# Attention and gated feed-forward on one core: the first head's probability sum gets a place of its own, the next tokens are prepared a unit earlier, two output tiles move into a batch's last unit, and the last key tile's denominators come from its probabilities

## The reference

```python
x = x + _attention(_tc_rmsnorm(x, t, g1w, g1b, b1w, b1b), Wq, Wk, Wv, Wo)
return x + _swiglu(_tc_rmsnorm(x, t, g2w, g2b, b2w, b2b), gate_w, hid_w, out_w)
# _tc_rmsnorm: g * x * rsqrt(mean(x * x) + EPS) + b, with g and b from t
# _attention: 16 heads of 32; softmax(q k / sqrt(32)) v, then Wo
# _swiglu: silu(x @ gate_w.T) * (x @ hid_w.T) @ out_w.T, hidden width 2048
```

## Time and profile before

| | |
|---|---|
| median of 3 runs | 2479.52 us (2472.38 to 2492.58) |
| the profiled execution | 2483.76 us, its span 2481.9 us |
| mean granted TensorE clock | 0.976 |
| busy share of the span | PE 93%, PEld 63%, DVE 68%, ACT 53%, POOL 59% |
| first exponential of batches 0 to 3 | 94.52, 445.95, 795.53, 1143.42 us |
| last exponential of batches 0 to 3 | 378.72, 730.17, 1078.31, 1423.99 us |

### The profile page before, as it was taken

The page is one execution under the profiler, slowest core; times in us unless marked ns, Lnnn a source line. Parts: engine busy times, 40 slices in busy tenths (PEclk is TensorE's granted clock), DMA queues, the critical chain, the costliest instruction groups (busy, mean ns, idle before and its releaser), DMA issues. The chain is left out here.

```text
span 2481.9 us, 40287 instructions
## 1 busy us (share of the span) xinstructions
PE 2309.7 (93%) x10884; PEld 1572.9 (63%) x10884; DVE 1676.2 (68%) x2732; ACT 1310.9 (53%) x2319; POOL 1454.4 (59%) x1351
## 2 busy tenths in 40 slices
PE   5999989999989999989999848999999999999999
PEld 4655436554447555456554336888888888888887
DVE  4776734667725776537777347887788778778877
ACT  3366762566752667734667724445444534454454
POOL 0388981689970888944889925731572166216711
PEclk8999999999989999999999978999999999999999
DMA  5212203212122122132222043115412541254125
GB/s 179 81 41 63 64 14 108 52 41 67 48 71 64 38 69 52 47 95 52 51 57 60 21 162 136 60 60 179 151 54 69 170 154 52 74 164 157 47 81 174
DMA packets 92656, 209.60 MB, mean 84 GB/s; under 512 B 15632, under 2 KB 15632, under 8 KB 90640
## 3 DMA queue, kind: packets, MB, share of 16 engines
q1 hardware_dynamic: 91344, 202.71, 27.2%
q0 software_dynamic: 1088, 4.19, 0.4%
HBM read 134.23 MB, written 19.92 MB: 62 GB/s over the span
## 5 line engine op out<-in xcount | busy, mean ns | idle before, releaser
L680 DVE TENSOR_REDUCE pmax<-bank 128x1 f32<-128x512 f32 x1024 | 653.7, 684 | 197.0 <-PE bank L893 187.6
L599 ACT ACTIVATE probs<-bank 128x512 f32<-128x512 f32 x1024 | 572.0, 600 | 330.6 <-PE bank L973 249.5
L447 POOL TENSOR_TENSOR sums<-sums,probs 128x512 f32<-128x512 f32 x512 | 641.4, 1291 | 0.5 <-ACT probs L599 0.5
L447 POOL TENSOR_TENSOR sums<-probs 128x512 f32<-128x512 f32 x256 | 320.4, 1282 | 380.6 <-ACT probs L599 258.9
L973 PE MATMUL bank<-qs,ks 128*128 128x512 f32 x1024 | 441.3, 439 | 40.0 <-ACT probs L599 37.9
L893 PE MATMUL bank<-ks,qs 96*128 96x512 f32 x1024 | 402.9, 406 | 25.8 <-DVE pmax L680 25.1
L973 PEld LDWEIGHTS bank<-qs,ks 128*128 128x128 f32 x1024 | 192.8, 191 | 323.4 <-ACT probs L599 167.3
L1536 PE MATMUL bank<-H_hi,wt_hi 128*128 128x512 f32 x896 | 350.0, 391 | 14.6 <-DVE H_lo L1391 14.6
L1550 PE MATMUL bank<-ow,aw 128*128 128x512 f32 x1536 | 358.7, 392 | 0.0
L1536 PE MATMUL bank<-H_lo,wt_hi 128*128 128x512 f32 x896 | 349.6, 390 | 0.0
L1536 PE MATMUL bank<-H_hi,wt_lo 128*128 128x512 f32 x896 | 349.5, 390 | 0.0
(11 more groups left out here) (139 smaller groups left out, 3233.8 us busy)
## 6 DMA issues: line engine op xcount, KB each, us to landing
raw<-in_gu_w SPq DMA_DIRECT2D x66, 512.0 KB, 3.6
wo_raw<-in_out_w SPq DMA_DIRECT2D x128, 256.0 KB, 2.6
ks<-qk_hi SPq DMA_DIRECT2D x136, 128.0 KB, 2.4
qs<-qk_hi SPq DMA_DIRECT2D x264, 64.0 KB, 2.0
x<-in_x SPq DMA_DIRECT2D x10, 1024.0 KB, 5.2
ks<-qk_lo SPq DMA_DIRECT2D x68, 128.0 KB, 2.4
qs<-qk_lo SPq DMA_DIRECT2D x132, 64.0 KB, 2.0
wv<-wv_parts SPq DMA_DIRECT2D x4, 2048.0 KB, 8.9
```

Source lines behind the costliest of these rows:

```text
L447: nc.gpsimd.tensor_tensor(sums[:, h, :], first, probs[:, s % 2, h, :], ALU.add) \
L599: nc.scalar.activation(probs[:, s % 2, h, :], sbank[i % SB][:], ACT.Exp, scale=SCALE).then_inc(st_done, 1)
L680: nc.vector.reduce_max(pmax[:, t, h, hf:hf + 1], mbank[n % MB][:], AX_X).then_inc(sq_done, 1)
```

## The change

Four things are changed.

1. `sum_place`: in the first half of a unit the first head's sum goes to `yout[:, 0]`, in the second half to `sums[:, 0]`; so the first addition of a half no longer writes what the denominator matmuls read, and the wait for them goes from the first head to the second. At a batch's start the first addition waits for the store of the output tile that lay in `yout[:, 0]`. The squares' unused output goes to `qk_hi` instead of `yout`.
2. The next tokens' load, squares, roots, scaling and transposes stand about a unit earlier, and the projections that are in their way are drawn together.
3. Tiles 0 and 1 of the output projection are made in unit 7, two matmuls a step from q = 18 and q = 24. For this VectorE, not GpSimd, multiplies unit 6's output, in unit 7 at (3, 0), from a copy of `den` in the free bank `mspare`; the first three tiles of `o` are copied to that bank before they are split.
4. Unit 7's last key tile is not added by GpSimd: the denominators are made from the sum of key tiles 4 to 6 and, by four more matmuls, from the probabilities of tile 7; they stand ahead of output tiles 2 to 7, and VectorE does unit 7's multiplication too.

```diff
-HT_AT = {5: (9, 13, 17, 24), 7: (13, 16, 19, 23)}
+HT_AT = {(4, 15): (0, 0), (4, 18): (1, 0), (4, 24): (2, 0), (5, 8): (3, 0),
+         (6, 14): (0, 1), (6, 17): (1, 1), (6, 24): (2, 1), (7, 0): (3, 1)}
+EARLY_OUT = {18: 0, 24: 1}
+SPLIT_AT = {(3, 3): 0, (4, 1): 1, (7, 1): 2}
...
+    def sum_place(quad, h):
+        return yout[:, 0, :] if (quad, h) == (0, 0) else sums[:, h, :]
+
...
-                    if u == 3:
+                    if u == 1:
                         load_x(b, 0, prepared)
...
-                hold(sp, held, sum_done, sums_done(b, NU - 1, NS - 1, GH - 1))
+                hold(sp, held, w_ready, MISC(b, misc_index(True, ("D", NU - 1, 1)) + 1))
                 load_wv()
...
-                        if (u, s) == (4, 5):
+                        if (u, s) == (3, 6):
                             inverse_root(b, b * 2 + 2)
-                        if (u, s) == (6, 6):
+                        if (u, s) == (6, 0):
                             inverse_root(b, b * 2 + 3)
-                        if s == 4 and u:
+                        if s == 4 and 0 < u < NU - 1:
                             normalise(b, u - 1)
+                        if n == NU * NS - 1:
+
+                            pool.wait_ge(sum_done, sums_done(b, u, s - 1, GH - 1))
+                            pool.sem_inc(sum_done, GH)
+                            break
...
-                            if s % QT == 1 and h == 0:
+                            if (u, s, h) == (0, 1, 0):
+
+                                pool.wait_ge(y_stored[0], b * (NT // 2 * 16) + 16)
+                            if s % QT == 1 and h == 1:
 
                                 pool.wait_ge(w_ready, MISC(b, sums_before(u, s // QT)))
...
-                            first = probs[:, 0, h, :] if s % QT == 1 else sums[:, h, :]
-                            nc.gpsimd.tensor_tensor(sums[:, h, :], first, probs[:, s % 2, h, :], ALU.add) \
+                            total = sum_place(s // QT, h)
+                            first = probs[:, 0, h, :] if s % QT == 1 else total
+                            nc.gpsimd.tensor_tensor(total, first, probs[:, s % 2, h, :], ALU.add) \
                                 .then_inc(sum_done, 1)
...
-                normalise(b, NU - 1)
...
+                tokens = o[:, :, t * P:(t + 1) * P]
+                if t in SPLIT_AT.values():
+                    up = mspare[:].rearrange("p (g c) -> p g c", g=NG)
+                    if t:
+                        act.wait_ge(os_dve, b * NT + t)
+                    nc.scalar.activation(up, tokens, ACT.Copy).then_inc(o_up, 1)
+                    act.wait_ge(o_up, b * len(SPLIT_AT) + (t + 1))
+                    tokens = up
+                nc.scalar.activation(osplit[:, t % 2, 0, :, :], tokens, ACT.Copy).then_inc(os_act, 1)
+
+            def denominators_up(b):
+
+                act.wait_ge(den_ready, b * (NU - 1) + (NU - 1))
+                act.wait_ge(sq_done, SCORES_Q(b, (NU - 1) * NMAX + NMAX) + MB)
+                nc.scalar.activation(mspare[:], den[:], ACT.Copy).then_inc(den_up, 1)
...
-                            if (u, s) == (4, 4):
+                            if (u, s) == (3, 4):
                                 square(b, 0, h)
-                            if (u, s) == (4, 6):
+                            if (u, s) == (4, 1):
                                 scale_x(b, 0, h)
-                            if (u, s) == (6, 3):
+                            if (u, s) == (5, 5):
                                 square(b, 1, h)
-                            if (u, s) == (6, 7):
+                            if (u, s) == (6, 2):
                                 scale_x(b, 1, h)
...
-                for t in range(2):
-                    lo_part(t)
                 out_tile(0)
-                for t in range(2, 4):
-                    lo_part(t)
+                lo_part(len(SPLIT_AT))
                 work_tile(b, ("D", NU - 1, 1))
-                for part in range(3):
+                for part in range(4):
                     normalise(b, NU - 1, part)
...
+                direct = (u, quad) == (NU - 1, QUADS - 1)
+                pe.wait_ge(sum_done, sums_done(b, u, QT * quad + QT - 1 - direct, GH - 1))
                 for h in range(GH):
-                    last = nc.tensor.matmul(wbank[DH * h:DH * h + DH, :], ones[:], sums[:, h, :], start=True, stop=True)
+                    last = nc.tensor.matmul(wbank[DH * h:DH * h + DH, :], ones[:], sum_place(quad, h), start=True,
+                                            stop=not direct)
+                for h in range(GH if direct else 0):
+                    last = nc.tensor.matmul(wbank[DH * h:DH * h + DH, :], ones[:], probs[:, (NS - 1) % 2, h, :], start=False,
+                                            stop=True)
...
+                            for q, t in EARLY_OUT.items() if u == NU - 1 else ():
+                                step = s * GH + h - q
+                                if 0 <= step < NG * 3 // 2:
+                                    out_tile(b, t, slice(2 * step, 2 * step + 2))
```

104 lines of the change are left out of this document (66 added, 38 removed).

## The result

The changed kernel takes 2487.2 us (median of 20 runs, 2478.7 to 2495.5), the kernel before 2478.2 (median of 20, 2472.4 to 2492.6). The ratio is 1.003, with a 95% interval of 1.0019 to 1.0041: the change costs 0.3%, where 2419 us had been forecast. The profiled execution has a span of 2483.8 us.

The account below looks back on a forecast made before the run. Took GpSimd's closed loop of additions and waits for denominator reads as the bound, with TensorE nearly full; 29 (units 0 to 6) + 11.7 (last unit) + 17.2 (end) + 2 (half clock), 60 us off 2479.5: 2419 us, range 2392 to 2452.

Parts of the forecast that it names:

- the part on the next tokens: Units 3 to 6: next tokens' work about a unit earlier wins 0.8 - 0.3 + 1.4 + 2.0 = 3.9 us per batch.
- rival 3: Units 5 and 6 fall to half clock (1.2 GHz), 16 us more per unit, 128 in four batches: 2547 us; chance 0.04.
- the steps on part 1: GpSimd's loop shortens 1.82 us per unit; units 0, 1, 2 win 0.5 + 1.5 + 1.35 = 3.35 us.
- TensorE can follow only as far as its idle time goes: Caps the 1.82 us won in GpSimd's loop at TensorE's idle time: 1.51, 1.35 and 1.52 us in units 1, 2, 3.
- the shifted tiles: In unit 7, two output tiles enter (5.54 us), three transposed tiles leave (2.0): 34.2 us against a mean of 37.1.
- a rule against the row: The skill's rule, optimize the highest-occupancy engine first, makes relieving GpSimd (59%) worth nothing: 2450 us; the rows say 2419.
- Unit 4: Gets back 1.02 us from the root, takes on three transposed tiles (2.0): -0.3 us, between +0.2 and -2.5.
- Unit 7 and the end: Last unit wins 2.9 us per batch (11.7 in all), the batch's end 4.3 (17.2), tile 5 starting about 744.6.
- Rival 1: TensorE is the floor in units 0 to 6; only last unit and end win, 29 us: 2450 us; chance 0.20.
- rival 2: Everything overlaps: units win 1.8 each, last unit 4, end 6.6, about 85 us: 2395 us; chance 0.13.
- a bound for units 0 to 6: Upper bound of 12.5 us per batch (50 in all), if the full 1.82 comes in each of seven units.

Follow-up runs that it names:

- e7: e1's kernel with the parts of the query projections in units 0 and 2 two heads apart, as before the change: 2417.7 us, ratio 0.975.
- e1: The changed kernel with the mean square made by ScalarE behind its fourth square instead of by VectorE: 2431.0 us, ratio 0.980.
- e5: The kernel before with only the first head's sum in its own place, in units 0 to 3, 5 and 7: 2445.3 us, ratio 0.987.
- e4: The changed kernel with the first head's sum in the common place again, waiting for the denominators ahead of each half's first addition: 2466.0 us, ratio 0.993.
- e2: The changed kernel with the mean square still on VectorE, same place and waits, but as a tensor_reduce over two numbers: 2433.4 us, ratio 0.980.
- e3: The changed kernel with GpSimd's two inverse roots one key tile earlier, VectorE's instructions untouched: 2447.3 us, ratio 0.987.
- e9: e7's kernel with the first half's transposed tiles split two in unit 4 and two in unit 5: 2417.4 us, ratio 0.976.
- e10: e7's kernel with the 2 MB load of wv in four parts, one behind each of the first four output stores: 2404.9 us, ratio 0.970.

## Why the prediction was wrong

In the table stand the mean lengths of the stretches over the batches in us, from the starts of exponentials and of the first copy of the values in the timelines (the end over three batches), and the length that each step of the prediction gives. Each column is one profiled execution, and a stretch at the lower clock in one batch moves a mean: unit 5 of e7 takes 35.2 us in batch 1, with 3.4 us at 1.2 GHz in it, and 34.0 in the mean.

```
stretch   before  forecast   after      e1      e7
unit 0     34.73      34.2   35.36   36.26   34.08
unit 1     34.94      33.4   33.15   33.14   33.14
unit 2     34.85      33.5   34.72   35.32   33.64
unit 3     34.95      34.1   38.86   33.19   33.16
unit 4     36.00      36.2   36.99   37.04   36.62
unit 5     34.88      33.5   40.13   34.34   33.96
unit 6     35.46      33.5   35.66   33.11   34.34
unit 7     37.12      34.2   32.39   32.42   32.40
end        31.31      27.0   28.28   26.03   27.02
```

**The step that failed** is in the part on the next tokens: "The squares, the mean square and one inverse root go from unit 4 to unit 3", costed at "1.82 won, 1.02 lost for the inverse root: 0.8". Of the moved things only the root had a price. The mean square had none, although its row, shown above, had 0.94 and 2.32 us where 0.17 was its length alone, and although GpSimd's root and SyncE's load of x had been counted. It measured 5.7 and 9.3 us, TensorE's standstills behind it 3.7 and 6.2. That is unit 3 at 38.9 instead of 34.1, and unit 5 at 40.1 instead of 33.5. With the stretches at 1.2 GHz it makes the 56 us between the changed kernel and e1. No rival was near it: rival 3 had the half clock as its mechanism, and the half clock came, but only for 6.8 to 10.2 us at a time, with a standstill, and not from fewer projections: e1 has as few of them in unit 5 and ran at 1.00 there in batch 1.

The failure is one of interaction, and part 1 and part 2 look blameless one by one. Part 1 alone wins 35 us (e5), and part 2 and the rest without it 14 (e4, 2480.4 to 2466.0). Together they lose 9. The gap that part 1 takes from GpSimd in unit 3 is the gap in which the mean square ended in e4. The prediction counted GpSimd's gaps as loss alone. That the multiply-add on VectorE, beside GpSimd's unbroken additions, is the cause is shown from three sides (e1, e2, e3). Why part 1 turns its length from 1.1 to 9.3 us in unit 5 is not: there was no gap at that point in e4 either, and it got the first turn there and none with part 1.

The Trainium skill, "SBUF — State Buffer", section "Who interferes with whom", says that VectorE and GpSimd share a second pair of ports as an exclusive lock, that a copy or a tensor_scalar on VectorE can want it, and that a tensor_reduce never does. The trace agrees on who waits: the multiply-add and the copy took up to 9.3 and 7.7 us, the reduction 0.15 to 0.16 us in the places of the mean square. The section also says that whoever issues first holds the pair for the whole instruction and the other is blocked; by that the mean square would have cost at most the rest of one addition, under 1.3 us, and as an estimate the sum would have moved by about 1 us per batch. There the trace differs: measured were up to eight additions, seven of which began after it.

**What was not priced at all:** the projections of queries one head apart. e7 puts it at 13 us of the kernel with the mean square on ScalarE, 2.2 us per batch in unit 0 and 1.7 in unit 2 (the profiles' means). In the forecast units 0 and 2 were to win 0.5 and 1.35; in e7 they win 0.65 and 1.2, so the steps on part 1 were about right there and this one was missing. The reason, as far as unit 0 shows it, is a place in `qk` that the stacking DMA had not yet left.

**Part 1.** "TensorE can follow only as far as its idle time goes", 1.5 us in unit 1: it followed by 1.8. The rule was too careful: the wait of 1.4 us went, and TensorE's busy time fell with it from 33.41 to 33.06 us, so idle time alone was not all that could be won. Unit 7 also gained 2.7 us from part 1 alone (e5), where the prediction gave the whole gain to the shifted tiles. And e5 answers what the prediction set as a rule against the row: GpSimd (59%) was not the engine with the largest share, and relieving GpSimd alone won 35 us. The prediction took TensorE for the engine that the shares name; by them VectorE (68%) stands above the weight loads (63%).

**Unit 4.** -0.3 was taken between +0.2 and -2.5; e7 gives -0.6 and the changed kernel -1.0. The wait for a transposed tile's split was there as foreseen (one of 0.98 us in e1), and e9 shows that the tiles cost the same where they are moved to.

**Unit 7 and the end.** Unit 7 won 4.7 us instead of 2.9: TensorE waited 0.53 us for tile 0's operand in batch 1, and the clock stayed at 1.00 there. The end of batch 1 came as foreseen, tile 5 at 744.60, and the late store was the reason; over the batches it won 3.0 us in the changed kernel and 4.3 in e7, the forecast's figure. e10 shows the load ahead of the stores to be worth another 2.6 us in batch 1 (3.7 in the mean of three, 12.8 us in the kernel's time).

**The sum.** e7 is the change as the prediction imagined it, without the two side effects. It takes 2417.7 us, where 2419 had been said. That is in part luck: unit 7 came out 1.8 us better than its step, and units 4, 5 and 6 together 1.7 worse. Rival 1, "TensorE is the floor", is refuted by unit 1 and by e5; rival 2, 2395, went too far by what units 0, 2, 4, 5 and 6 and the end (4.3 instead of 6.6) did not give. The gain of 12.5 us per batch that the prediction names as a bound for units 0 to 6 is 12.7 by its own terms (seven times 1.82), which changes nothing.

## What to carry to other kernels

When a change fills the gaps of GpSimd, list every VectorE multiply-add and copy from SBUF to SBUF beside it, however small, and look at its longest duration in the trace and not its mean: 2.3 us for four numbers per partition was the warning. The form matters more than the size: in the changed kernel the transposes of `den`, SBUF to SBUF and 128x512, kept their 0.70 to 0.71 us and the reciprocals their 0.24 to 0.26, beside the same additions. The cheapest cure here was to give the small operation to ScalarE or to write it as a tensor_reduce. Judge the parts of a change together where one removes the idle time in which another's work was hidden, and price each place that a moved step takes over from a DMA.
